# Two fused attention layers on one core: another order of the output projection, the input projection and the first transposed probabilities on TensorE

## What is computed

```
q = (xn @ Wq).reshape(b, n, HEADS, DIM_HEAD).transpose(0, 2, 1, 3)
kv = xn @ Wkv
...
q = l2norm(q) * q_scale
k = l2norm(k) * k_scale
sim = jnp.einsum('bhid,bjd->bhij', q, k) * SCALE
...
attn = jax.nn.softmax(sim, axis=-1)
out = jnp.einsum('bhij,bjd->bhid', attn, v)
out = out.transpose(0, 2, 1, 3).reshape(b, n, HEADS * DIM_HEAD)
return ln(out @ Wout, g_out)
```

## Time and profile before

| | before |
|---|---|
| median of the runs | 2398.06 us (2397.39 to 2398.73) |
| profiled execution | 2398.48 us |
| its span | 2396.7 us |
| TensorE, matmuls | 2328.6 us busy, 97% |
| VectorE | 1614.6 us busy, 67% |
| ScalarE | 1597.0 us busy, 67% |
| GpSimd | 900.6 us busy, 38% |
| mean granted TensorE clock | 0.99 |

### The profile page before, as it was taken

How to read it: one execution, slowest core, us unless ns; L and a number is a source line. 1 busy time by engine, 2 the same in 40 slices (tenths; PEclk the granted TensorE clock), 3 DMA queues, 4 the chain that set the end, 5 groups by cost and what they waited for, 6 DMA issues and landing times.

```text
span 2396.7 us, 55136 instructions
## 1 busy us (share of the span) xinstructions
PE 2328.6 (97%) x17435; PEld 2041.2 (85%) x17435; DVE 1614.6 (67%) x4513; ACT 1597.0 (67%) x6497; POOL 900.6 (38%) x1688
## 2 busy tenths in 40 slices
PE   2899999999999999999999999999999999999998
PEld 1788888888888888888888888888888888888877
DVE  5376676676676676766666766766766666766666
ACT  4466666676666676666666666666666666666766
POOL 1234334334334334334334334434433434433432
PEclk7899999999999999999999999999999999999999
DMA  6111111111211111111111111111111111111111
GB/s 224 36 48 53 60 43 48 55 46 52 60 43 47 55 46 52 59 45 47 55 46 52 56 47 47 55 46 52 55 46 50 56 42 55 52 45 54 57 35 41
DMA packets 108835, 129.50 MB, mean 54 GB/s; under 512 B 47072, under 2 KB 51200, under 8 KB 108800
## 3 DMA queue, kind: packets, MB, share of 16 engines
q1 hardware_dynamic: 105888, 127.68, 17.3%
q10 hardware_dynamic: 2912, 1.38, 0.2%
HBM read 81.79 MB, written 33.57 MB: 48 GB/s over the span
## 4 chain that ended last, share of the span: by engine, by line
PE 96%; DVE 1%; ACT 0%; POOL 0%; issue 0%; POOLq 0%; DVEq 0%
PE psum L589 30%; PE psum L485 17%; PE psum L453 15%; PE psum L575 10%; PE psum L541 10%; PE psum L552 6%; PE psum L415 3%; PE psum L502 2%; PE psum L464 2%; PE psum L472 0%; PE psum L493 0%; ACT probs L681 0%; POOL weights L900 0%; POOL masked_bias L887 0%; DVE neg_max L813 0%
## 5 line engine op out<-in xcount | busy, mean ns | idle before, releaser
L900 POOL TENSOR_TENSOR weights<-probs,den_inv 128x256 f32<-128x256 f32 (+3 forms) x1024 | 470.8, 487 | 1416.3 <-DVE den_inv L819 1412.5
L681 ACT ACTIVATE probs<-probs,neg_max 128x129 f32<-128x129 f32 (+3 forms) x2048 | 715.9, 352 | 310.5 <-DVE neg_max L813 310.5
L806 DVE TENSOR_TENSOR probs<-psum,masked_bias 128x324 f32<-128x324 f32 x512 | 225.7, 483 | 282.5 <-PE psum L541 281.4
L887 POOL TENSOR_TENSOR masked_bias<-bias,pad_neg 128x516 f32<-128x516 f32 (+3 forms) x512 | 394.3, 803 | 13.4 <-POOL pad_neg L883 4.5
L681 ACT ACTIVATION_READ_ACCUMULATOR probs<-probs,neg_max 128x1 f32 x2048 | 385.3, 188 | 0.0
L589 PE MATMUL psum<-wo_hi,o_hi 128*128 128x512 f32 x1024 | 271.4, 407 | 0.8 <-issue 0.8
L589 PE MATMUL psum<-wo_hi,o_lo 128*128 128x512 f32 x1024 | 267.7, 404 | 0.0
L813 DVE TENSOR_REDUCE neg_max<-probs 128x2 f32<-128x258 f32 (+3 forms) x1024 | 256.9, 313 | 4.5
L589 PE MATMUL psum<-wo_lo,o_hi 128*128 128x512 f32 x1024 | 259.3, 396 | 0.0
L688 ACT COPY probs_t<-psum 128x384 f32<-128x384 f32 (+1 forms) x512 | 192.2, 428 | 76.7 <-PE psum L552 76.5
L589 PEld LDWEIGHTS psum<-wo_lo,o_hi 128*128 128x128 f32 x1024 | 193.0, 188 | 45.9
(11 more groups left out here) (132 smaller groups left out, 4379.3 us busy)
## 6 DMA issues: line engine op xcount, KB each, us to landing
res<-in_x_dram SPq DMA_DIRECT2D x64, 256.0 KB, 2.7
x_of<-y_out SPq DMA_DIRECT2D x64, 256.0 KB, 2.0
res<-x_of SPq DMA_DIRECT2D x64, 256.0 KB, 2.7
out_dram<-y_out SPq DMA_DIRECT2D x64, 256.0 KB, 2.0
xa<-in_x_dram SPq DMA_DIRECT2D x63, 256.0 KB, 2.7
xa<-x_of SPq DMA_DIRECT2D x63, 256.0 KB, 2.8
q_aside<-qp SPq DMA_DIRECT2D x32, 256.0 KB, 2.9
w_raw<-in_L_cond_Wq_dram SPq DMA_DIRECT2D x8, 512.0 KB, 7.5
```

Of the source, the lines that this page charges most:

```text
L681: x_ = nc.scalar.activation(s, s, ACT.Exp, bias=neg_max[:, g, k, e:e + 1], accum_out=den[:, g, k, e:e + 1])
L806: a = nc.vector.tensor_tensor(probs[:, 2 * c + e, :], SB[c][e][:, 0:ROW], masked_bias[:, 2 * c + e, :], ALU.add)
L887: m = nc.gpsimd.tensor_tensor(block(masked_bias, b), block(bias[u.layer], b), pad_neg[u.layer][:, 0:WIDTH[b]].unsqueeze(1).to_broadcast([P ...
L900: m = nc.gpsimd.tensor_tensor(places[b], block(pairs(probs, g // 2), b)[:, :, 1:1 + n], den_inv[:, g, k, :].unsqueeze(2).to_broadcast([P, ...
```

## The change

In `late`, on TensorE alone, the third part of the output projection moves from between the two pairs of transposed probabilities to just behind the first two parts. The input projection now gets its banks as an argument: banks 2 and 0 come first, then the transposed probabilities of groups 0 and 1, then bank 1, then those of groups 2 and 3.

```diff
-            def project(w, u):
-                for b in (2, 0, 1):
+            def project(w, u, banks):
+                for b in banks:
...
             def late(u, v, w, n, loads, then, pairs_done):
                 run_stages((part(scores, 0), u), (part(scores, 1), u), (part(transpose_second, pairs_done), w),
-                           (part(project_out, 0), v), (part(project_out, 1), v), (part(project, u), w), (part(transpose_p, (0, 1)), u),
-                           (part(project_out, 2), v), (part(transpose_p, (2, 3)), u), (transpose_k, w), (transpose_q, w), (values, u))
+                           (part(project_out, 0), v), (part(project_out, 1), v), (part(project_out, 2), v),
+                           (part(project, u, (2, 0)), w), (part(transpose_p, (0, 1)), u), (part(project, u, (1,)), w),
+                           (part(transpose_p, (2, 3)), u), (transpose_k, w), (transpose_q, w), (values, u))
```

## The result

The changed kernel takes 2574.93 us (two runs, 2574.49 to 2575.36) against 2398.06 us before: 1.0733 times as long, 95% interval 1.0707 to 1.0759. The forecast was 2577 us, between 2530 and 2640. The profiled execution spans 2572.7 us, 176.0 us more than before.

The account below looks back on a forecast made before the run. PE (TensorE) bounds the kernel, busy 2328.6 of 2396.7 us with no slack between slots. 2398.5 us before + 144 us waiting for bank 1's chain + 35 us of clock falls = 2577 us, range 2530 to 2640.

Parts of the forecast that it names:

- The frame: On TensorE: busy 2328.6 of 2396.7 us without slack between slots, so any new wait adds in full, once per slot.
- Step (c): Input projection on PE: bank 1 ends behind the moved part and first transposes, so its square starts 2.41 us later.
- step (e): Bank 1's square to transposed queries: chain end plus 0.14 us to PE makes queries 2.27 us late, 2.24 in another slot.
- The term: Loss from bank 1's chain over all slots: 64 x 2.25 = 144 us, bounds 129 and 156.
- Step (d): Second transposes on PE wait for ScalarE's first copy: a first gap of 1.4 us, inside the chain and not added.
- The second gap: On PE between the key's transposition and the transposed queries: some 0.7 us of waiting per slot.
- Step (b): Bank 2 and ScalarE work behind it come about 1.9 us later; nothing on PE waits; uncovered, a few tenths.
- Step (f): Values, split of o and next scores move with the transposed queries; nothing else is late behind the chain.
- Step (g): Three slots without an input projection: PE waited for POOL anyway, so 0, bounds -1 to +2 us in all.
- Step (h): PE's granted clock falls after gaps in a third of the slots, 1.6 us each: 35 us, possible 0 to 104.

Follow-up runs that it names:

- e4: Changed kernel with eight throwaway matmuls added on PE, six ahead of the second transposes and two ahead of the transposed queries: 2546.47 us, ratio 1.0617.
- e3: Changed kernel with ScalarE's copies of the first transposed probabilities moved ahead of the square of bank 1: 2570.46 us, ratio 1.0717.
- e9: Changed kernel with the third output-projection part moved behind banks 2 and 0, ahead of the first transposes and bank 1: 2576.58 us, ratio 1.0742.
- e5: Changed kernel without bank 1's square, norms and inverse root, bank 1 scaled by bank 0's factors (wrong queries): 2450.25 us, ratio 1.0220.
- e2: Kernel before with only the first transposed probabilities moved ahead of bank 1, third output-projection part between bank 1 and second transposes: 2425.40 us, ratio 1.0113.
- e1: Kernel before with only the third output-projection part moved ahead of the input projection, first transposes still behind bank 1: 2515.96 us, ratio 1.0490.

## Why the prediction was right

- The frame (PE full, every new wait paid once a slot) held. PE shows no other new wait in the slots.
- Step (c), bank 1 later by 2.41 us, and step (e), the chain of 2.73 us and a loss of 2.27 and 2.24 us: the chain measured 2.73 us, and the slots at full clock grew by 2.30 us (14.19 us before from the first part of the output projection at 1238.15 to the values at 1252.34; 16.49 us after). The term was 144 us; e4, which has the term alone, measured 148 us. It is 3% short: the transposed queries came 2.26 us later (15.49 us behind the first part of the output projection, 13.23 before), as forecast, and the values another 0.04 us behind them.
- Step (d), the first gap of 1.4 us inside the chain: 1.47 us, and e3 shows that it isn't added. The agreement is closer than the step. PE's second transposes start 0.60 us behind the start of the copies (1338.11 to 1338.71) and not 0.4, so by starts, as the step counts, the gap is 1.6 us; the profile counts it from the modelled end of the last matmul. The second gap, forecast as 0.7 us, is smaller by that: the transposed queries start 0.73 us behind the key's transposition, and 0.11 us of that is PE's own pace. The waits show 0.46 us of it. The sum of the two is set by the chain, so the time doesn't depend on how it is divided.
- Step (b) said that nothing on PE waits for what stands behind bank 2. In the changed kernel that is so (e9). Its price "if the cover fails", a few tenths, was too low: the cover is the chain itself, and e5, which took it away, paid 1.0 us in every second slot. The queue of VectorE in the slots with a normalisation had not been followed.
- Step (f), nothing late next: no wait appeared at the scores, the output projection or the values. The price of the first transposes' place alone (e2) and of the third part alone (e1) came out within 2 us or so of the same kind of sum, though these two were written down with the trace of the changed kernel at hand.
- Step (g), the slots without an input projection: the trace shows 0 to within 0.2 us. From the last transposed queries to the end of the span it is 28.0 us in both kernels (from 2368.73 before, from 2544.70 after). Around the slot of A(63), from one transposed queries to the next, it is 35.19 us before (2296.70 to 2331.89) and 38.90 after (2464.48 to 2503.38): 3.7 us more, of which 2.3 are the wait of the slot behind it and 1.6 one of the 18 falls. The fall of the earlier trace rows is there in both.
- Step (h), the clock: 35 us from falls in a third of the slots (21) at 1.6 us each; measured 18 falls at 1.62 us, 29 us, and 28.5 us less by e4. The price rested on rows. The share did not: it was a guess between two cases, and that it came so close is luck. The sentence after the Trainium skill ("TensorE: Matmul & The Clock Gate", section "A second HAM failure mode: psum-queue depth-cycling"), by which short idles in every iteration set the clock swinging, is borne out here for the changed kernel and not for e1, which has shorter idles in every slot and a full clock.
- 147 + 29 = 176 us is the whole difference of the two spans. So no step on which the forecast rests failed; what was guessed and not worked out is the share of the slots in (h).

## What to carry to other kernels

Ahead of moving work on the bound engine, ask what it was covering: take the last thing that starts a chain over other engines and the first that needs its end, and compare the chain with what the bound engine has to do between them. Here PE had work for 2.87 us between the start of the square and the transposed queries, over a chain of 2.73, and each tenth taken away beyond that was paid 64 times, which made the loss predictable from four rows of the trace. And the largest wait of a profile isn't the one to mend if it ends inside a longer chain: e3 removed 95 us of it and won 4.5.

## What was not expected of the hardware

Gaps shorter than the 2.28 us of the earlier trace rows were enough. Two gaps of 1.47 and 0.46 us, with six transposes between, came with a fall in 18 of 64 slots; a single gap of 1.98 us behind six transposes (e3) in 21; gaps of 1.0 and 0.46 us with the same six transposes between (e1) in none, though there the five first transposes stand ahead of the gaps as well. The slots hit do the same work as the others. In each of the 18 the clock falls within 0.7 us behind the start of the transposed queries, and from one fall to the next it is always 78.5, 116.1 or 269.7 us. So the slots hit look to be picked by their timing and not by what they do; no run here tests that. For a kernel with a periodic gap near this size the clock's share has to be measured: useless matmuls in the gap (e4) cost nothing and gave 28.5 us back.
